# Attention kernel product of an image tower: high and low kernel columns side by side in one product, with a new order of calls

## The reference, cut to what matters

```python
def tower(x):
    h = patchify(x) @ tok_W.T + tok_b               # 196 tokens x 256
    h = h + attention(layernorm(h))
    return h + tree_ffn(layernorm(h))

def attention(x):
    xn = x / max(norm(x) * D ** -0.5, eps) * g
    uv = silu(xn @ uv_w.T)                          # u: 512, v: 512, base: 128
    q, k = rope(base * gamma + beta)                # each 196 x 128
    kernel = square(relu((q @ k.T + w_rel[j - i]) / sqrt(128)))   # 196 x 196
    out = u * (kernel @ v)                          # the product that is changed
    return x * res_scale + out @ o_w.T

def tree_ffn(x):                                    # 8 trees, 255 nodes each
    logits = x @ W_in.T + b_in
    acts = silu(logits), kept only for the nodes on the path that the signs choose
    return acts @ W_out.T
```

## Time and profile before

| what | value |
|---|---|
| median of 3 runs | 2263.17 us (2258.26 to 2264.08) |
| profiled execution, its own time | 2262.11 us |
| its span, first to last instruction | 2260.3 us |
| PE busy with matmuls | 2204.4 us (98%), 13248 of them |
| DVE busy | 1721.6 us (76%) |
| ACT busy | 1091.2 us (48%) |
| POOL busy | 292.8 us (13%) |
| mean granted TensorE clock | 0.991 of full speed |

### The profile page before, as it was taken

How to read it: one execution, slowest core, us unless ns; L and a number is a source line. 1 busy time by engine, 2 the same in 40 slices (tenths; PEclk the granted TensorE clock), 3 DMA queues, 4 the chain that set the end, 5 groups by cost and what they waited for, 6 DMA issues and landing times.

```text
span 2260.3 us, 37987 instructions
## 1 busy us (share of the span) xinstructions
PE 2204.4 (98%) x13248; PEld 2078.2 (92%) x13248; DVE 1721.6 (76%) x3534; ACT 1091.2 (48%) x1992; POOL 292.8 (13%) x361
## 2 busy tenths in 40 slices
PE   6799999999999999999999999999999999999999
PEld 5799999999999999999999999999999999999998
DVE  5677787778787777877777877787777778777876
ACT  4344554444554445544445544445444455444453
POOL 4631111001111001110011110011100111100110
PEclk8899999999999999999999999999999999999999
DMA  3110000000000000000000000000000000000000
GB/s 115 53 45 9 21 28 28 28 28 0 28 28 28 28 14 14 28 28 28 28 0 28 28 28 28 18 11 28 28 28 28 0 28 28 28 28 21 7 18 15
DMA packets 38403, 58.89 MB, mean 26 GB/s; under 512 B 4879, under 2 KB 32497, under 8 KB 38385
## 3 DMA queue, kind: packets, MB, share of 16 engines
q1 hardware_dynamic: 38384, 58.66, 8.8%
HBM read 45.80 MB, written 12.85 MB: 26 GB/s over the span
## 4 chain that ended last, share of the span: by engine, by line
PE 86%; DVE 8%; issue 3%; ACT 2%; POOL 1%; DMA 0%; DVEq 0%; SPq 0%; ACTq 0%; POOLq 0%
PE front L904 11%; PE front L906 11%; PE front L905 11%; PE out_acc L904 8%; PE hid_ps L904 8%; PE hid_ps L905 8%; PE hid_ps L906 8%; PE out_acc L905 8%; PE out_acc L906 8%; PE front L939 3%; PE front L932 3%; DVE tok_major L689 2%; PE hid_ps L1080 2%; DVE tok_major L257 2%; DVE v_lo L593 1%
## 5 line engine op out<-in xcount | busy, mean ns | idle before, releaser
L904 PE MATMUL hid_ps<-ffn_x,in_lo 128*128 128x392 f32 x1024 | 368.4, 360 | 5.3 <-POOL in_lo L338 4.1
L904 PE MATMUL out_acc<-hid_hi,outw_lo 128*128 128x392 f32 x1024 | 367.4, 359 | 0.0
L905 PE MATMUL hid_ps<-ffn_x,in_hi 128*128 128x392 f32 x1024 | 350.9, 343 | 0.0
L906 PE MATMUL hid_ps<-ffn_x,in_hi 128*128 128x392 f32 x1024 | 350.2, 342 | 0.0
L905 PE MATMUL out_acc<-hid_lo,outw_hi 128*128 128x392 f32 x1024 | 348.8, 341 | 0.0
L906 PE MATMUL out_acc<-hid_hi,outw_hi 128*128 128x392 f32 x1024 | 348.5, 340 | 0.0
L498 ACT ACTIVATE hid<-hid_ps,leaf_col 128x392 f32<-128x392 f32 x256 | 149.3, 583 | 357.1 <-PE hid_ps L906 315.6
L344 POOL TENSOR_TENSOR inv_root<-to_root,minus_half 98x8 f32<-98x8 f32 x64 | 106.3, 1661 | 1609.6 <-DVE to_root L633 918.6
L773 DVE SCALAR_TENSOR_TENSOR hid<-hid_ps,hid 128x392 f32<-128x392 f32 x512 | 261.7, 558 | 40.9 <-PE hid_ps L1080 40.9
L382 ACT ACTIVATE hid_hi<-hid 128x784 fp32r<-128x784 f32 x256 | 219.6, 858 | 151.1 <-PE out_acc L906 113.5
L593 DVE TENSOR_TENSOR hid_lo<-hid,hid_hi 128x784 fp32r<-128x784 f32 x256 | 248.3, 970 | 17.2 <-ACT hid_hi L382 17.2
(11 more groups left out here) (111 smaller groups left out, 4924.3 us busy)
## 6 DMA issues: line engine op xcount, KB each, us to landing
x_raw<-x SPq DMA_DIRECT2D x192, 196.0 KB, 2.4
out<-out_stage SPq DMA_DIRECT2D x32, 392.0 KB, 2.4
late_raw<-in_w SPq DMA_DIRECT2D x8, 256.0 KB, 2.8
late_raw<-out_w SPq DMA_DIRECT2D x8, 128.0 KB
tok_major<-tok_w SPq DMA_DIRECT2D x3, 256.0 KB, 4.7
u<-uv_w SPq DMA_DIRECT2D x1, 576.0 KB, 4.4
late_raw<-o_w SPq DMA_DIRECT2D x2, 256.0 KB, 5.3
late_raw<-out_w SPq DMA_DIRECT2D x8, 64.0 KB
```

Source lines behind the costliest of these rows:

```text
L904: pe.matmul(out, w[1], x_parts[0], start=start, stop=False)
L905: pe.matmul(out, w[0], x_parts[1], start=False, stop=False)
L906: return pe.matmul(out, w[0], x_parts[0], start=False, stop=stop)
```

## The change

Seven things change. The list of blank lines and unchanged calls is cut.

1. `mix` is called eight times in a unit, once for each channel group e and image m. A call issues four matmuls: high v x (high and low kernel side by side, 392 columns), low v x high kernel (196 columns) for the first half of the keys, the same two for the second half in reverse order. Columns 0 to 195 of the bank hold all that belongs to the high kernel, columns 196 to 391 the high v x low kernel part.
2. `copy_mix` on ACT copies the second half of the bank (196 columns) into SBUF (`mix_sum`, which reuses `base` and `base_sw`), and `sum_mix` on DVE adds the first half of the bank to it. Both run eight times in a unit.
3. `gate` reads `mix_sum` and no longer PSUM.
4. The bank of a `mix` step is free with the `sum_mix` of the step two before; `copy_mix` of groups 2 and 3 waits for the `gate` two before.
5. On PE, `tree_visits` 0, 3, 6 and 7 come earlier, 4 later, `tree_logits(i, 5, 0)` moves behind the four `make_v`, and `tree_out(i, 0, 0)` before `tree_logits(i, 3, 1)`.
6. On DVE, `decisions(i, 4)` comes before the residual and `mask(i, 3)` after `hid_low(i, 2)`, directly ahead of `swap_base`; `qk_low`, `v_low`, `decisions` and `hid_low` change places at some points; the one-time `build_toward` and `uv_low` come later.
7. On ACT, `v_high(n, 2)` comes before `silu_v(n, 3)`, `hid_high(i, 3)` behind two `silu_v`, and `silu_u(n, 0)` and `(n, 1)` before `silu_tree(i, 4, 1)`; the order at the start of a unit changes as well.

The number of `tree_visits` in a unit stays one for each tree.

```diff
@@ -72,7 +72,7 @@
...
 BANK_QK = (1, 0)
-BANK_MIX = (1, 0) * (EC // 2)
+BANK_KV = (1, 0) * EC
 BANK_O = (1, 0)
...
@@ -150,6 +150,7 @@
...
+        mix_sum = [base, base_sw]
         u_t = u[:, :].rearrange("p (e t) -> p e t", e=EC)
...
@@ -201,7 +202,7 @@
...
         kern_hi_ok, kern_lo_ok = sem("kern_hi_ok"), sem("kern_lo_ok")
-        mixed, gated = sem("mixed"), sem("gated")
+        mixed, mix_copied, summed, gated = sem("mixed"), sem("mix_copied"), sem("summed"), sem("gated")
         mix_hi_ok, mix_lo_ok = sem("mix_hi_ok"), sem("mix_lo_ok")
...
@@ -459,6 +460,17 @@
...
+            def copy_mix(n, step):
+
+                if n is None:
+                    return
+                e, m = step // PAIR, step % PAIR
+                act.wait_ge(mixed, EC * PAIR * n + step + 1)
+                if m == 0 and e >= 2:
+                    act.wait_ge(gated, EC * n + e - 1)
+                act.activation(mix_sum[e % 2][:, m * L:(m + 1) * L], front[:, BANK_KV[step], L:2 * L],
+                               ACT.Copy).then_inc(mix_copied, 1)
+
             def mix_high(n, e):
...
@@ -509,22 +521,22 @@
...
                 x_high(n, 1)
+                x_high(n, 2)
                 silu_tree(i, 0, 1)
-                x_high(n, 2)
                 silu_tree(i, 0, 0)
+                silu_tree(i, 1, 1)
                 x_high(n, 3)
...
                 x_high(n, 5)
+                silu_tree(i, 1, 0)
+                hid_high(i, 0)
+                copy_h(n, 0)
+                copy_h(n, 1)
+                hid_high(i, 1)
                 if first(n):
                     uv_high((0,))
-                silu_tree(i, 1, 1)
-                hid_high(i, 0)
-                silu_tree(i, 1, 0)
-                copy_h(n, 0)
-                copy_h(n, 1)
                 if first(n):
                     uv_high((1, 2))
-                hid_high(i, 1)
                 silu_tree(i, 2, 1)
...
@@ -537,34 +549,42 @@
...
                 silu_base(n)
-                hid_high(i, 3)
                 silu_v(n, 0)
                 silu_v(n, 1)
+                hid_high(i, 3)
                 v_high(n, 0)
...
                 silu_v(n, 2)
+                v_high(n, 2)
                 silu_v(n, 3)
                 qk_high(n, 1)
+                silu_u(n, 0)
+                silu_u(n, 1)
+                v_high(n, 3)
                 silu_tree(i, 4, 1)
-                silu_u(n, 0)
                 silu_tree(i, 4, 0)
-                silu_u(n, 1)
-                v_high(n, 2)
                 silu_tree(i, 5, 1)
...
                 kern_high(n, 0)
-                v_high(n, 3)
                 kern_high(n, 1)
...
                 silu_u(n, 3)
+                copy_mix(n, 0)
+                copy_mix(n, 1)
                 hid_high(i, 4)
+                copy_mix(n, 2)
+                copy_mix(n, 3)
+                copy_mix(n, 4)
+                copy_mix(n, 5)
                 mix_high(n, 0)
-                silu_tree(i, 6, 1)
                 mix_high(n, 1)
                 mix_high(n, 2)
+                copy_mix(n, 6)
+                copy_mix(n, 7)
+                silu_tree(i, 6, 1)
+                mix_high(n, 3)
                 silu_tree(i, 6, 0)
-                mix_high(n, 3)
                 hid_high(i, 5)
...
@@ -692,6 +712,8 @@
...
                     return
+                if first(n):
+                    dve.wait_ge(tables_in, TABLE_DMAS * 16)
                 rotate(dve, n, 0, q_step)
...
@@ -727,12 +749,21 @@
...
+            def sum_mix(n, step):
+
+                if n is None:
+                    return
+                e, m = step // PAIR, step % PAIR
+                dve.wait_ge(mix_copied, EC * PAIR * n + step + 1)
+                part = mix_sum[e % 2][:, m * L:(m + 1) * L]
+                dve.tensor_tensor(part, front[:, BANK_KV[step], 0:L], part, ALU.add).then_inc(summed, 1)
+
             def gate(n, e):
...
                     return
-                dve.wait_ge(mixed, EC * n + e + 1)
-                dve.scalar_tensor_tensor(u_t[:, e], front[:, BANK_MIX[e], 0:T], 1.0 / S, u_t[:, e],
+                dve.wait_ge(summed, PAIR * (EC * n + e + 1))
+                dve.scalar_tensor_tensor(u_t[:, e], mix_sum[e % 2][:, :], 1.0 / S, u_t[:, e],
                                          ALU.mult, ALU.mult).then_inc(gated, 1)
...
@@ -808,24 +839,24 @@
...
                 decisions(i, 0)
+                x_low(n, 2)
                 decisions(i, 1)
-                x_low(n, 2)
+                mask(i, 0)
                 x_low(n, 3)
                 x_low(n, 4)
-                mask(i, 0)
                 x_low(n, 5)
-                if first(n):
-                    uv_low((0,))
                 hid_low(i, 0)
                 mask(i, 1)
-                decisions(i, 2)
                 norm_stats(n, 0, 0)
...
                 norm_moments(n, 0)
+                decisions(i, 2)
+                hid_low(i, 1)
+                decisions(i, 3)
+                if first(n):
+                    uv_low((0,))
                 if first(n):
                     uv_low((1, 2))
-                hid_low(i, 1)
-                decisions(i, 3)
                 norm_apply(n, 0, 0)
...
@@ -833,46 +864,54 @@
...
                 xn_low(n, 0)
                 xn_low(n, 1)
+                decisions(i, 4)
                 residual(n, 0)
-                mask(i, 3)
                 residual(n, 1)
                 hid_low(i, 2)
-                if first(n):
-                    build_toward()
+                mask(i, 3)
                 swap_base(n)
                 scale_base(n, 1)
...
                 v_low(n, 0)
                 v_low(n, 1)
-                decisions(i, 4)
                 qk_low(n, 0)
+                v_low(n, 2)
+                qk_low(n, 1)
                 decisions(i, 5)
-                qk_low(n, 1)
+                if first(n):
+                    build_toward()
                 hid_low(i, 3)
                 add_rel_bias(n, 0)
                 square_relu(n, 0)
-                v_low(n, 2)
                 add_rel_bias(n, 1)
                 square_relu(n, 1)
+                v_low(n, 3)
                 kern_low(n, 0)
-                v_low(n, 3)
                 kern_low(n, 1)
                 mask(i, 4)
                 mask(i, 5)
+                sum_mix(n, 0)
+                sum_mix(n, 1)
+                hid_low(i, 4)
+                sum_mix(n, 2)
                 gate(n, 0)
-                hid_low(i, 4)
+                sum_mix(n, 3)
+                decisions(i, 6)
                 gate(n, 1)
-                decisions(i, 6)
+                sum_mix(n, 4)
+                sum_mix(n, 5)
+                gate(n, 2)
                 mix_low(n, 0)
-                gate(n, 2)
                 mix_low(n, 1)
                 mix_low(n, 2)
+                sum_mix(n, 6)
+                sum_mix(n, 7)
                 gate(n, 3)
+                mix_low(n, 3)
+                hid_low(i, 5)
+                update_h(n, 0)
                 decisions(i, 7)
-                mix_low(n, 3)
-                update_h(n, 0)
-                hid_low(i, 5)
                 update_h(n, 1)
                 mask(i, 6)
...
@@ -1014,25 +1053,27 @@
...
-            def mix(n, e):
-
-
-                if n is None:
-                    return
-                if e == 0:
+            def mix(n, step):
+
+
+                if n is None:
+                    return
+                e, m = step // PAIR, step % PAIR
+                if step == 0:
+                    pe.wait_ge(v_lo_ok, GROUPS * (n + 1))
                     pe.wait_ge(kern_lo_ok, PAIR * (n + 1))
-                if e < 2:
-                    pe.wait_ge(u_ok, EC * n + e + 3)
+                if step < 2:
+                    pe.wait_ge(u_ok, EC * n + step + 3)
                 else:
-                    pe.wait_ge(gated, EC * n + e - 1)
+                    pe.wait_ge(summed, EC * PAIR * n + step - 1)
+                bank = front[:, BANK_KV[step]]
                 at = slice(e * P, (e + 1) * P)
-                for m in range(PAIR):
-                    for j in range(2):
-                        parts = [kern_parts[:, m, j, p] for p in range(2)]
-                        last = product(front[:, BANK_MIX[e], m * L:(m + 1) * L],
-                                       [v[:, 2 * m + j, at] for v in (v_hi, v_lo)], parts,
-                                       j == 0, j == 1)
-                last.then_inc(mixed, 1)
+                both = [kern_parts[:, m, j].rearrange("p a l -> p (a l)") for j in range(2)]
+                pe.matmul(bank[:, 0:2 * L], v_hi[:, 2 * m, at], both[0], start=True, stop=False)
+                pe.matmul(bank[:, 0:L], v_lo[:, 2 * m, at], kern_parts[:, m, 0, 0], start=False, stop=False)
+                pe.matmul(bank[:, 0:L], v_lo[:, 2 * m + 1, at], kern_parts[:, m, 1, 0], start=False, stop=False)
+                pe.matmul(bank[:, 0:2 * L], v_hi[:, 2 * m + 1, at], both[1],
+                          start=False, stop=True).then_inc(mixed, 1)
```

(26 more changed lines are left out.)

## The result

The changed kernel takes 2268.38 us (median of 20 runs, 2265.70 to 2270.02), the kernel before 2263.25 us (median of 20). The ratio is 1.0022, with a 95% interval of 1.0016 to 1.0028: slower by 5 us, inside the 0.3% that the prediction named as hard to tell from no change. The profiled execution spans 2267.5 us where that of before spans 2260.3; these two lie 7.2 us apart, not 5.1, since the one of before ran 1.1 us under its median and the other (2269.5 us) 1.1 us over its own.

What follows compares the result with a forecast made beforehand. PE's issued work in a unit plus its stall for v_full bound the kernel; 2262.1 - 23.6 (product) + 27.0 (stall) + 1.6 (rest of the order) = 2267.1 us. Its own range was 2258 to 2276, the overall range 2249 to 2284.

Steps and rivals of the forecast that it cites:

- The bound: PE in the joint units: time is what PE issues in a unit plus one stall of 0.77 us for v_full.
- The product: Kernel-v matmuls on PE: two steps take 1.15 us where a mix took 1.34, saving 23.6 us in all.
- Rival C: Kernel-v matmuls on PE: wide matmuls gain nothing because 98 rows set the pace; 2291 us, chance 4%.
- D: Weight loads on PE: loads were in the open, 16 of 0.11 us a unit saved; 2236 us, chance 1%.
- The stall: PE's wait for v_full: mask(3) delays swap_base on DVE, the stall goes from 0.77 to 1.64 us, 27.0 us added.
- The decisive row: DVE's wait for the base ahead of swap_base: once in the span, 1.6 us, so never early in joint units.
- Rival A: Chain to silu_v(2): it doesn't lengthen because DVE catches up before it; 2240 us, chance 12%.
- The copies and sums: Eight ACT copies and DVE additions a unit: 0.33 and 0.37 us each, hand-over costs nothing, covered by tree calls.
- Rival B: sum_mix of steps 2 to 5: bank hand-over stalls PE from 0.2 us of delay on; 2283 us, chance 20%.
- The rest: make_u(1) and scores(0) after the stall: inputs just ready or late, 0.05 us a unit, 1.6 us in all.
- The first unit: One-time build_toward and uv_low move into DVE idle time, mixes take about the same: 0, between -3 and +3 us.

Runs made afterwards that it cites:

- e1: The kernel before with only mask(i, 3) moved on DVE behind hid_low(i, 2), directly ahead of swap_base; 2289.6 us, ratio 1.0116.
- e2: The changed kernel with mask(i, 3) and decisions(i, 4) put back to their old places on DVE; 2244.5 us, ratio 0.9914 to the kernel before.
- e3: The kernel before with only the new kernel-v product and the call order between the first mix and tree_logits(7, 0); 2241.4 us, ratio 0.9904.
- e4: The kernel before with 98 instead of 128 weight columns in each mix matmul, leaving part of the product out; 2227.8 us, ratio 0.9844.
- e10: The changed kernel with only decisions(i, 4) put back behind v_low(n, 1) on DVE; 2269.3 us, ratio 1.0021 to the kernel before.
- e5: e3 with v_low(0) and v_low(1) ahead of rotate_q on DVE and other calls reordered; 2244.3 us, ratio 0.9914 to the kernel before.
- e9: e5 with v_low(3) moved earlier on DVE and silu_u(0), silu_u(1) earlier on ACT; 2221.2 us, ratio 0.9807 to the kernel before.
- e7: e3 with three extra short ACT copies ahead of each copy_mix, each copy 0.19 us later; 2243.5 us, ratio 0.9909 to the kernel before.
- e8: The changed kernel with the one-time uv_high(0) and uv_low(0) put back to their old places; one execution, span 2267.4 us.

## Why the prediction was right

**The bound.** PE's work in a unit and one stall make the time: e1, e2 and e3 changed one of the two each and came within 4 us of the times forecast for them.

**The product.** 0.76 us a unit were forecast, 0.72 are in the changed kernel's rows (4 x (1.34 - 1.16)) and 0.73 in e3's unit. The reading behind it, that loads of 128 columns set the pace of short matmuls, is shown by e4. Rival C (no gain) and D (loads in the open, 55 us) are refuted by e3: 22 us.

**The stall.** 0.87 us a unit were forecast, 0.88 are seen (1.65 - 0.77), 0.86 in e1. The decisive row was the one that did not occur: no wait for the base ahead of `swap_base` in a joint unit. e10 confirms that `decisions(4)` is hidden. Rival A, DVE catching up, is refuted by e1.

**The copies and sums.** 0.33 and 0.37 us were estimated for 196 columns; the page has 330 to 334 ns on ACT and 355 to 358 ns on DVE. Cover by the tree calls held in every joint unit but the first, where PE waited 0.4 us once. Rival B did not occur. The slack behind this was mis-sized, on the safe side: 0.57 us at step 5 and not 0.2, so that B's threshold of 0.2 us of delay was too low.

**The rest.** 0.05 us a unit were taken for `make_u(1)` and `scores(0)`: 0.08 at `make_u(1)`. The sum by measured terms is -0.72 + 0.88 + 0.08 = 0.24 us a unit; the units differ by 0.20 to 0.21.

**The first unit.** Priced at nothing, between -3 and +3 us. `turn_xn` came 1.5 us later and the eight steps took 50.68 to 60.29, 9.6 us where the earlier trace rows has 8.35, so the first `project_o` stood 2.9 us later. At the second `make_u(0)` the changed kernel was 0.3 us ahead again (116.86 against 117.17), but PE had waited 3.48 us for `v_full` there, and in the next 3.34 us the granted clock was 0.52 of full speed, near the lower of its two levels (1.2 of 2.4 GHz), where that of before was 1.00 at the same place: matmuls of 392 columns stand 0.33 apart.

```profile
113.04 0.34 PE L945 MATMUL out_acc<-hid_hi,outw_hi 128*128 128x392 f32 x1
116.86 0.69 PE L943 MATMUL front<-xn,uv_lo 128*128 128x392 f32 x1 [3.48 <-ACT v_full L437]
...
117.68 0.53 PE L945 MATMUL front<-xn,uv_hi 128*128 128x392 f32 x1
118.01 0.53 PE L943 MATMUL front<-xn,uv_lo 128*128 128x392 f32 x1
```

The unit that begins there takes 72.05 us where that of before takes 69.56, 2.5 more and not 0.2. The prediction has no term for this. This unit is 3.0 us longer than the later ones in the changed kernel, in e2 and in e10, 0.7 before and in e1, and 1.1 in e3, so most of it belongs to the rest of the new order; which call makes it is not shown. The fallen clock is in it: nine matmuls 0.33 apart and not 0.18 are 1.4 us, and in e2 the granted clock fell to 0.58 at this place too, after a wait of 2.81 us. The rest of the 3.0 us stays open. From the third `make_u(0)` on, 2.2 us behind, 29 units of 0.20 add 5.8 us, and the end gives 0.75 back: the 7.2 us between the spans. Start and end together come to about 1 us beyond the 31 x 0.2 of the units. That is within the stated range, but as a sum of larger parts of both signs, which is luck. That `uv_low` would stand beside GpSimd's power operation, which then takes 3.92 us and not 2.66, was missed: I called that time idle on DVE and did not ask what GpSimd did.

The total, 2267.1, lies 1.3 us under the measured median, and 1.1 of this is the starting point, an execution 1.1 us under its median. The forecast rise of 5.0 us and the measured one of 5.1 agree more closely than the terms do: the product saved 22.3 us and not 23.6, the stall cost 27.3 and not 27.0, the rest of the order 2.5 and not 1.6, which makes 7.5. So the two large terms were right within 6%, and the agreement within 0.1 us is luck.

## What to carry to other kernels

A saving on the engine that bounds the kernel and a call moved on another can cancel; price each by itself, for a sum near zero hides a gain worth keeping. Here 22 us of the changed kernel were good and 27 us were one call ahead of a chain that had no slack. Look in the waits for the place where a supporting engine is never early, and see whether the bounding engine waits at the end of the chain behind it: here a call of 0.94 us put ahead of that place cost 0.88 us a unit. And when a stall is taken away, look for the next one at once: e5 lost all it gained to two calls in the wrong place, and e9 got it back by order alone.

## What was not expected of the hardware

Very short ACT copies from PSUM follow each other every 0.063 us (three in 0.19 us in e7), while one with 196 columns takes 0.33 us on the page; the page's duration is no measure of what one more short operation costs.

GpSimd's power operation on 98 x 8 elements took 2.66 us in the first unit of e8, where DVE ran two subtractions of 576 columns with two SBUF inputs beside it, and 3.92 us in the changed kernel, where one of 1152 columns came ahead of those two. The same operation takes 2.29 us in every joint unit before and 1.64 us in every joint unit of the changed kernel, although `hid_low(1)`, a subtraction of 784 columns with two SBUF inputs, runs beside it in both. What differs is the start: before, `hid_low(1)` started 0.17 us ahead of GpSimd's operation (1201.82 against 1201.99); in the changed kernel it starts 0.40 us behind it (1206.65 against 1206.25), because `decisions(2)`, which reads PSUM, now stands ahead. DVE's wait for the result falls from 33.5 to 2.7 us in all. e3, with the old order, has 2.29 again, so the order makes the difference; that it is the order of these two starts was not tested by itself.

```profile
1206.25 1.64 POOL L345 TENSOR_TENSOR inv_root<-to_root,minus_half 98x8 f32<-98x8 f32 x1 [22.35 <-DVE to_root L663]
1201.99 2.29 POOL L344 TENSOR_TENSOR inv_root<-to_root,minus_half 98x8 f32<-98x8 f32 x1 [22.34 <-DVE to_root L643]
```

The first row is from the changed kernel, the second from the one before.
